# A decoder layer's recurrence on one Trainium2 core: two projections ahead of the sums, and the norm's small steps on VectorE

## What is computed

```python
x = resid * rsqrt(mean(resid * resid) + EPS) * norm_w
skip = x @ skip_w.T
x = silu(conv(x @ in_w.T) + conv_b)
delta = softplus(x @ Wd1.T @ Wd2_w.T + Wd2_b)
Bm, Cm = x @ WB.T, x @ WC.T
# for every token, 512 channels e and 16 states n:
h = exp(d_l[:, :, None] * A) * h + (d_l * x_l)[:, :, None] * B_l[:, None, :]
y_l = einsum('ben,bn->be', h, C_l)
# after it:
y = (y + x * W_D) * silu(skip)
x = layernorm(x + resid + y @ out_w.T)
```

## Time and profile before

| | us |
|---|---|
| median of 3 runs | 1883.05 |
| lowest and highest run | 1880.05, 1884.74 |
| the profiled execution | 1880.88, its span 1879.1 |
| the recurrence's loop | 47 to 909 of the span |
| next phase begins | 927 |

### The profile page before, as it was taken

The page is one execution under the profiler, slowest core; times in us unless marked ns, Lnnn a source line. Parts: engine busy times, 40 slices in busy tenths (PEclk is TensorE's granted clock), DMA queues, the critical chain, the costliest instruction groups (busy, mean ns, idle before and its releaser), DMA issues. The chain is left out here.

```text
span 1879.1 us, 32964 instructions
## 1 busy us (share of the span) xinstructions
PE 1625.9 (87%) x9680; PEld 1053.9 (56%) x9681; DVE 1452.1 (77%) x2270; ACT 1137.6 (61%) x2662; POOL 1241.9 (66%) x920
## 2 busy tenths in 40 slices
PE   8788888787888878884589999998999999999997
PEld 5455544454555544552256666665776555555686
DVE  6899999999999999999758888887533444444488
ACT  5778888888888888886335555564322333333325
POOL 2999999999999999999556888873401333333300
PEclk9899999999998899996679999999999999999999
DMA  8645455544454554445247755542264222222272
GB/s 234 145 105 125 113 135 136 124 109 104 103 127 113 136 136 117 110 100 120 77 114 170 197 183 159 152 143 74 81 234 157 85 85 85 87 86 84 72 269 90
DMA packets 179286, 238.30 MB, mean 127 GB/s; under 512 B 24714, under 2 KB 115725, under 8 KB 177070
## 3 DMA queue, kind: packets, MB, share of 16 engines
q1 hardware_dynamic: 160606, 200.64, 41.2%
q0 software_dynamic: 9888, 27.80, 4.2%
q10 hardware_dynamic: 8656, 8.18, 1.6%
HBM read 172.15 MB, written 65.90 MB: 127 GB/s over the span
## 5 line engine op out<-in xcount | busy, mean ns | idle before, releaser
L760 DVE TENSOR_TENSOR_SCAN ps_h<-ps_h,inject 128x1024 f32<-128x1024 f32 x160 | 365.4, 2284 | 27.7 <-ACT ps_h L589 27.4
L376 POOL TENSOR_TENSOR inject<-common,bc_n 128x2048 f32<-128x2048 f32 x63 | 285.5, 4544 | 60.7 <-issue 60.7
L376 POOL TENSOR_TENSOR inject<-dx_n,bc_n 128x2048 f32<-128x2048 f32 x64 | 290.4, 4551 | 0.0
L1537 ACT ACTIVATE expT<-ps_t 128x512 f32<-128x512 f32 x256 | 147.1, 593 | 164.5 <-PE ps_t L2042 164.4
L589 ACT ACTIVATE ps_h<-common,a_neg 128x256 f32<-128x256 f32 x512 | 211.4, 462 | 44.3 <-DVE hc L773 33.1
L760 DVE TENSOR_TENSOR_SCAN h_pool<-ps_h,inject 128x1024 f32<-128x1024 f32 x96 | 218.9, 2281 | 15.4 <-ACT ps_h L589 12.3
L589 ACT ACTIVATE ps_h<-delta_n,a_neg 128x256 f32<-128x256 f32 x512 | 212.7, 461 | 27.5 <-DVE hc L773 22.9
L1690 DVE TENSOR_REDUCE neg_max<-ps_s 128x2 f32<-128x512 f32 x256 | 173.4, 682 | 71.6 <-PE ps_s L2031 70.9
L385 POOL TENSOR_TENSOR h_pool<-h_pool,bc_n 128x1024 f32<-128x1024 f32 x96 | 227.0, 2365 | 0.0
L2696 PE MATMUL ps_uh<-arena,s_xT 128*128 x440 | 210.1, 600 | 4.7 <-issue 4.6
L2400 POOL DMA_INDIRECT token_results<-common,e_y_row x82 | 80.1, 976 | 190.6 <-DVE common L2549 190.6
(11 more groups left out here) (344 smaller groups left out, 3610.6 us busy)
## 6 DMA issues: line engine op xcount, KB each, us to landing
common<-dup_rows SPq DMA_DIRECT2D x120, 256.0 KB, 5.8
bc_n<-bc_rows SPq DMA_DIRECT2D x64, 256.0 KB, 4.7
delta_n<-dup_rows SPq DMA_DIRECT2D x64, 256.0 KB, 4.3
dx_n<-dup_rows SPq DMA_DIRECT2D x64, 256.0 KB, 7.4
arena<-slot_rows SPq DMA_DIRECT2D x110, 136.0 KB, 2.1
arena<-token_results SPq DMA_DIRECT2D x8, 1536.0 KB, 18.6
dup_rows<-delta SPq DMA_DIRECT2D x32, 256.0 KB, 3.6
dup_rows<-dx SPq DMA_DIRECT2D x32, 256.0 KB, 3.8
```

The source lines that it names most:

```text
L376: nc.gpsimd.tensor_tensor(inject[:, at:at + 2, :, :], dx_n[c // 2][:, None, :, c % 2, :].to_broadcast([P, 2, JB, L]), bc_n[b % 2][:, 0, nq ...
L760: nc.vector.tensor_tensor_scan(out.rearrange("p j t -> p (j t)"), ps_h[k % 2][:, :, :].rearrange("p j t -> p (j t)"), inject[:, k % RING, ...
L1537: nc.scalar.activation(expT[:, h % (2 * HG), :, :], ps_t[h % 2][:, :, :], ACT.Exp).then_inc(h_exp, 1)
```

## The change

- TensorE: project_db(b + 1) at step 4 is issued ahead of sums(b, 4). project_skip(b + 2, 1) at step 14 is issued ahead of sums(b, 14); the first half stays behind sums at step 13.
- ScalarE: the second take_skip moves from step 15 to step 0 of the following sequence, behind make_decay of that step.
- The norm: ScalarE keeps the copy, the log and the exponential at the same steps, and normalize. VectorE takes var + eps (step 7), r0 * r0 (10), times var (11), 1.5 - 0.5 of it (12), times r0 (13), and -mean * r2 (14), each one instruction on both columns, each waiting on row_step for the one in front of it, the one at 10 on root_step for the exponential. Each follows scan, gate and weigh of its step. The constants that ScalarE needed, and the copy of -mean, go. The wait of row_mean on ScalarE's reading of the sequence before goes too.
- Behind the loop the steps run in this order for the last sequence, across both engines.

```diff
@@ counters
-        STATS, MEAN = range(1, 3)
-        RES, VAR, LOG, ROOT, VR, VRR, OFF, INV, SHIFT = range(1, 10)
+        STATS, MEAN, VAR, RR, VRR, NEWTON, INV, SHIFT = range(1, 9)
+        RES, LOG, ROOT = range(1, 4)
@@ ScalarE
-            rows = {4: take_res, 7: row_var, 8: row_log, 9: row_root, 10: row_vr, 11: row_vrr, 12: row_off,
-                    13: row_scale, 14: row_shift, 15: normalize}
+            rows = {4: take_res, 8: row_log, 9: row_root, 15: normalize}
...
-                if entry and i in (14, 15):
-                    take_skip(b + 2, i - 14)
+                if entry and i == 14:
+                    take_skip(b + 2, 0)
+                if front and tail and i == 0:
+                    take_skip(b + 1, 1)
@@ VectorE
             def row_mean(b):
                 v.wait_ge(row_step, row(b, STATS))
-                if b >= 1:
-                    v.wait_ge(root_step, norm(b - 1, VAR))
                 for s in range(TT):
                     last = nc.vector.bn_aggr(mv[:, s, :], stats[:, s, :])
                 last.then_inc(row_step, 1)
+
+            def row_var(b):
+                v.wait_ge(row_step, row(b, MEAN))
+                nc.vector.tensor_scalar(var[:, :], mv[:, :, 1], EPS / 4.0, None, ALU.add).then_inc(row_step, 1)
+
+            def root_square(b):
+                v.wait_ge(root_step, norm(b, ROOT))
+                nc.vector.tensor_tensor(rr[:, :], r0[:, :], r0[:, :], ALU.mult).then_inc(row_step, 1)
+
+            def times_var(b):
+                v.wait_ge(row_step, row(b, RR))
+                nc.vector.tensor_tensor(vrr[:, :], rr[:, :], var[:, :], ALU.mult).then_inc(row_step, 1)
+
+            def newton(b):
+                v.wait_ge(row_step, row(b, VRR))
+                nc.vector.tensor_scalar(newton_r[:, :], vrr[:, :], -0.5, 1.5, ALU.mult, ALU.add).then_inc(row_step, 1)
+
+            def row_scale(b):
+                v.wait_ge(row_step, row(b, NEWTON))
+                nc.vector.tensor_tensor(r2[:, :], newton_r[:, :], r0[:, :], ALU.mult).then_inc(row_step, 1)
+
+            def row_shift(b):
+                v.wait_ge(row_step, row(b, INV))
+                nc.vector.scalar_tensor_tensor(shift[:, :], mv[:, :, 0], -1.0, r2[:, :], ALU.mult,
+                                               ALU.mult).then_inc(row_step, 1)
...
+            rows = {5: row_stats, 6: row_mean, 7: row_var, 10: root_square, 11: times_var, 12: newton, 13: row_scale,
+                    14: row_shift}
...
-                if b > 0 and i == 5:
-                    row_stats(b - 1)
-                if b > 0 and i == 6:
-                    row_mean(b - 1)
+                if b > 0 and i in rows:
+                    rows[i](b - 1)
@@ TensorE
+                if front and i == 4:
+                    project_db(b + 1)
+                if entry and i == 14:
+                    project_skip(b + 2, 1)
                 sums(b, i)
...
-                if front and i == 4:
-                    project_db(b + 1)
...
-                if entry and i in (13, 14):
-                    project_skip(b + 2, i - 13)
+                if entry and i == 13:
+                    project_skip(b + 2, 0)
```

More of the change, by code:

```diff
@@ L136, in mamba_phase @@
         mv = sb("mv", [P, TT, 2])
-        var, ln_var, r0, vr, vrr, half_off, r2, minus_mean, shift = (
-            sb(n, [P, TT]) for n in ("var", "ln_var", "r0", "vr", "vrr", "half_off", "r2", "minus_mean", "shift"))
-        ln_eps, one_half = sb("ln_eps", [P, 1]), sb("one_half", [P, 1])
+        var, ln_var, r0, rr, vrr, newton_r, r2, shift = (
+            sb(n, [P, TT]) for n in ("var", "ln_var", "r0", "rr", "vrr", "newton_r", "r2", "shift"))
         ps_h = [ps(f"ps_h{j}", [P, JB, L]) for j in range(2)]
@@ L164, in mamba_phase @@
             sem("t_" + n) for n in ("gated", "out", "row_step", "root_step", "x"))
-        STATS, MEAN = range(1, 3)
-        RES, VAR, LOG, ROOT, VR, VRR, OFF, INV, SHIFT = range(1, 10)
+        STATS, MEAN, VAR, RR, VRR, NEWTON, INV, SHIFT = range(1, 9)
+        RES, LOG, ROOT = range(1, 4)
         def row(b, step):
-            return b * MEAN + step
+            return b * SHIFT + step
         def norm(b, step):
-            return b * SHIFT + step
+            return b * ROOT + step
         def by_pool(k):
@@ L522, in take_res @@
                 nc.scalar.activation(res[:, :, :], ps_y[1][:, :, :], ACT.Copy).then_inc(root_step, 1)
[L524 to L527, removed]
             def row_log(b):
-                act.wait_ge(root_step, norm(b, VAR))
+                act.wait_ge(row_step, row(b, VAR))
                 nc.scalar.activation(ln_var[:, :], var[:, :], ACT.Ln).then_inc(root_step, 1)
@@ L535, in row_root @@
                 nc.scalar.activation(r0[:, :], ln_var[:, :], ACT.Exp, scale=-0.5).then_inc(root_step, 1)
[L537 to L562, removed]
             def normalize(b):
-                act.wait_ge(root_step, norm(b, SHIFT))
+                act.wait_ge(row_step, row(b, SHIFT))
                 for s in range(TT):
@@ L708, in _ @@
             refine(FIRST, 0)
-            nc.vector.memset(ln_eps[:, :], EPS / 4.0)
-            nc.vector.memset(one_half[:, :], 0.5)
             nc.vector.tensor_scalar(half_ident[:, :], ident[:, :], 0.5, None, ALU.mult)
@@ L844, in _ @@
                 split(q_rows[n], q_parts[n], 18 + 4 * (AHEAD + n), qk.q_split)
-            row_stats(B - 1)
-            row_mean(B - 1)
+            for step in rows.values():
+                step(B - 1)
         @block.tensor
```

## The result

| | us |
|---|---|
| before, median | 1881.97 (1880.05 to 1884.74, 4 runs) |
| changed kernel, median | 2004.08 (1993.91 to 2016.28, 4 runs) |
| ratio, 95% interval | 1.065, 1.0585 to 1.0716 |
| profiled execution, changed kernel | 1999.63, span 1997.8 |

A forecast was written before the change was run, and what follows sets the result against it. VectorE was taken to bound the recurrence, only its idle time winnable: 20.2 us of waits removed plus 1.7 at the last norm less 7.2 for small steps, 14.7 us less, median 1868 us, range 1861 to 1880.

The forecast's parts named there:

- wait A: VectorE's wait for ScalarE's decay ahead of step 2's scan in nine sequences; 10.6 us in sum, all forecast to go.
- wait B: VectorE's wait for ScalarE ahead of step 5's scan, sequences 1 to 14; 22.4 us, 4.1 to go, floor 1.31 each.
- rival 3: Step 6's gate waits for sums now behind db; at TensorE's lower clock 21 us lost, 1889; chance 0.07.
- The small steps: Six norm instructions added to VectorE at steps 7 and 10 to 14, 90 in the loop; 0.08 us each, 7.2 cost.
- the upper bound: High end for each small VectorE step, 0.20 us, if each needs the one in front; 18 us for 90.
- The last norm: Last sequence's norm, serial behind the loop: 3.5 us on ScalarE ahead of normalize, forecast 1.7 us shorter.
- take ScalarE's place: Rival 1: GpSimd's injections hold the scans, wait A returns as a wait for inject; 4.1 us gained, 1879; chance 0.12.
- reserve at step 2: Time by which GpSimd's injection ends ahead of step 2's scan; forecast 0.14 to 1.24 us once wait A is gone.
- rival 2: The small VectorE steps cost the dependent distance, 18 us instead of 7.2, giving 1879; chance 0.08.

## Why the prediction was wrong

- **What bounds the kernel: right**, and the sum that rests on it. With the moves alone wait A went whole, wait B to its floor of 1.31 us, and the time fell by 20.3 us (forecast 20.2), so near in part by luck. In the changed kernel the waits fell by 20.1 us, but with the norm's steps alone they fell by 16.4.
- **Each move as a term of its own: wrong.** The sum held only for both. The skip move alone lost 0.8% where its terms (10.6 + 4.1) said 14.7 us less. They took db as it was in the rows, 1.97 us long and covered ("the next decays have enough reserve"); with that move it started later and took 2.9 to 3.7 us in ten sequences, in part or whole at the lower clock level, which the prediction weighed in rival 3 alone.
- **The small steps: wrong, and by the order of magnitude.** The step that failed is "what counts is the distance from its start to the next start", read at 8.58 us, where GpSimd does nothing, and at 1022.48, which has one column. In the loop of before GpSimd is busy 93% of the time, 82% in the changed kernel's, and 90 steps took 142.4 us (149.6 less the overlap), 1.58 each: neither the 0.08 taken nor the 0.20 of the upper bound. The bounds were bounds of the instruction alone. What another engine has under way was not in them.
- The trace of before did hold a case. VectorE's queue has one two-column instruction in the loop that reads SBUF only, bq times a constant in sequence 0. It lasts 0.73 us, and GpSimd's product beside it ends 0.02 us ahead of it (before, VectorE then GpSimd):

```profile
104.68 0.73 DVE L835 TENSOR_SCALAR bq<-bq 128x2 f32<-128x2 f32 x1
```

```profile
103.04 2.35 POOL L385 TENSOR_TENSOR h_pool<-h_pool,bc_n 128x1024 f32<-128x1024 f32 x1
```

  The rest of VectorE's work in that loop, scans, products, gates, dx, reads at most one tensor from SBUF and the other from PSUM, and the statistics read one. I had seen 0.73 for a shape that took 0.17 elsewhere, and took no note. In the traces of the other kernels the same instruction lasts 0.16 to 0.94 us, by how long GpSimd's product beside it has to go.
- **What was weighed against the change was the wrong thing.** The prediction asked whether one small instruction puts the next one off by 0.09 or by 0.16 us, which decides between 7 and 14 us; the wait for GpSimd decided 135.
- **The last norm: right.** 1037.16 to 1038.85 against 3.5 us before, 1.8 us gained (forecast 1.7).
- **The rivals.** GpSimd did not take ScalarE's place, though its reserve at step 2 fell to 0.09 us with the moves alone. The dependent distance (rival 2) had the right part of the change and an eighth of its size (18 us of 142). Gates waiting behind db (rival 3) did not happen. No rival had GpSimd hold VectorE.

## What to carry to other kernels

Before putting an instruction on VectorE beside a busy GpSimd, count its tensor reads from SBUF: two inputs in SBUF, or a fp32 tensor_scalar of two or three columns, stood until a GpSimd instruction was through, however small they were, while one-column tensor_scalars did not; so price it from a row in a stretch in which GpSimd works. A short instruction with an odd duration is worth a look at what the other engines end at that moment, since such a wait is booked as busy time. And a wait taken out of one queue can leave another engine idle for longer, which here made its next matmuls both late and slow: cost moves together, and try them one by one.

## What the runs showed of the hardware that was not expected

- A two-column VectorE instruction of 0.15 to 0.17 us lasted up to 7.2 us behind GpSimd's tensor_tensor in the changed kernel, and up to 8.1 with halved injections. GpSimd's own instructions did not get longer: 4.54 us for an injection in both kernels.
- The wait need not end with the GpSimd instruction under way. In the kernel with halved injections every var lasted through two to four of them, until GpSimd stopped for want of a scan. Why var misses the seams is open.
- The granted clock of TensorE over the loop was 0.87 of full speed in the changed kernel, where TensorE was busy 74% of the time, 0.93 with the moves alone (80%) and 0.91 before (79%). No part of the difference between these three is put down to it. In the kernel with the skip move alone the eight matmuls of db took 1.97 us in four of sequences 1 to 14 and 2.9 to 3.7 in ten.
